# A weight fetch for a change of expert at step 23 moved to step 1 in a mixture-of-experts stage

## The chip, the cores and the metric

The kernel runs on one core of a Trainium2 chip, in one launch. The metric is the device time of that launch in microseconds (us). Below, PE is TensorE, DVE is VectorE, ACT is ScalarE, POOL is GpSimd and SP is SyncE, which in this kernel only issues transfers and waits.

## The reference, cut to what matters

The layer is a graph-attention stage, a linear-attention stage, and a mixture-of-experts (MoE) stage on 1250 rows of 768 columns. Only the last one matters here:

```python
probs = softmax(x @ router_w)                    # 8 experts
gates, idx = top_k(probs, 2)                     # 2 experts for each row
g = silu(x @ w_gate[e]);  u = x @ w_up[e]        # for every expert e, 768x768 each
expert_out = (g * u) @ w_down[e]
routed = sum over the two experts of gate * expert_out
shared = silu(x @ ws_gate) * (x @ ws_up) @ ws_down
out = x + alpha * shared + (1 - alpha) * routed
```

## The kernel before

The MoE stage works in 23 steps (`NTM`), numbered 0 to 22. The rows are sorted by expert into chunks of 64 slots, and each step takes two chunks at once, one in each half of the PE array. Half 0 runs through the experts from the front (it starts with expert 0), half 1 from the back (it starts with expert 7). Each half has its own set of three weight buffers of 2304 KB (gate, up, down): `ew[0][i]` and `ew[1][i]`, at the arena offsets `EW[i][0]` and `EW[i][1]`. The first six weights are fetched by `load_expert` (L616) while the shared part runs.

There are always seven changes of expert (`NB1`). DVE works out a table of them while the shared part runs: in `order_changes` it has for each change the step from which the new weights are needed (`cht`), the expert (`che`) and the half (`isr`), ranks the changes by step, and counts for each step how many changes are due by then. `list_changes` writes that count as `loads_i` (32 + 16 for each change due) and the sorted list as `change_i`, three rows of seven integers, in a loop of one pass per row (L1097 to L1101). PE takes `loads_i[j]` at the start of step j and waits for that value of `s_ew[0]` ahead of the gate products, `s_ew[1]` ahead of the up products, and `s_ew[2]` ahead of the down products; `s_ew[i]` rises by 16 with each landed weight of kind i.

A change whose `cht` is 23 belongs to a boundary between experts that falls right behind the last step of half 0. No step needs its weights, but they are fetched all the same, and waited for at the end of SP's program.

The order on SP, an in-order queue, is: the loads of the first weights, mixed with the stores of the ten groups of output rows (`store_rows`, L372; semaphore `s_fout`), two small loads of the slot table (L640, L641), the wait for `s_et` (the table of changes is there), and then the loop over the seven changes (L645 to L653). Each turn loads three integers into registers (L646 to L648), and for gate, up and down in turn waits for the weights of the turn before and for PE to have done with the old ones (L651: `s_g`, `s_up` or `s_y` at `at_step`), and issues the fetch (L652). Behind the loop SP waits for all weights, for `s_fout` and for the last row write.

POOL adds each chunk's rows into the output in DRAM: an indirect read of 64 rows (L690), DVE adds the products (L1156), an indirect write (L694), one chunk after the other, 46 in all but the last two, which share one read (L698) and one write (L701). DVE works in order too: `take_h(j+1)` (L1143), which PE needs for the turns (L797) in step j+1, stands behind the two `add_rows` of step j. The PE lines are L803 for all expert products (48 matmuls for each of gate, up, down as the trace counts them), L788 for the turns of x, L797 for the turns of h, L841 for the last step.

Of the kernel before, what the change touches and what calls it, by code (L numbers as in the profile page):

```python
# [24 lines left out]
I32 = mybir.dt.int32  # L25
U32 = mybir.dt.uint32
U16 = mybir.dt.uint16
ALU = mybir.AluOpType
# [7 lines left out]
ARENA = 52900  # L36
SMALL = 3456
# [19 lines left out]
def gps_layer(nc, x, src, dst, norm_g, norm_b, W1, a_src1, a_dst1, b1, W2, a_src2, a_dst2, b2, Wu, bu,  # L57
              w_qkv, w_proj, b_proj, router_w, w_gate, w_up, w_down, ws_gate, ws_up, ws_down, sg_w, sg_b,
              out):
    N, D = x.shape  # L60
    KD = D // P
    NT = 10
# [16 lines left out]
    NTM = -(-((2 * N + NE * (HP - 1)) // HP) // 2)  # L79
# [3 lines left out]
    with ExitStack() as ctx:  # L83
        def sem(name):
            return ctx.enter_context(nc.semaphore(name))

        arena = ctx.enter_context(nc.sbuf_tensor("arena", [P, ARENA], F32))
        ps = [ctx.enter_context(nc.psum_tensor(f"bank{i}", [P, 512], F32)) for i in range(8)]

        def words(off, n, dt=F32):  # L90
            v = arena[:, off:off + n]
            return v if dt == F32 else v.bitcast(dt)

        def region(at, size):

            pos = [SMALL + at]

            def take(n, dt=F32):
                w = n if dt in (F32, I32, U32) else (n + 1) // 2
                v = words(pos[0], w, dt)  # L100
                pos[0] += w
                assert pos[0] <= SMALL + at + size and pos[0] <= ARENA, (at, size, pos)
                return v
            return take
# [64 lines left out]
        COUNTS, MASK, V12, MIXT, XNT, ZB, END = 0, 6256, 12506, 20426, 27926, 35426, ARENA - SMALL  # L169
# [133 lines left out]
        EWW = KD * D  # L303
        EW = [(SMALL + WBO + i * EWW, SMALL + w) for i, w in enumerate((0, EWW, V12 + NT * D + KD * N + KD * HG - EWW))]
        assert NT * D <= 2 * EWW <= NT * D + KD * HS and 6 * D <= KD * N + KD * HG - EWW
        ew = [[words(EW[i][b], EWW).rearrange("p (k n) -> p k n", k=KD) for i in range(3)] for b in range(2)]
        sg_s = words(EW[2][0], NT * HS).rearrange("p (t n) -> p t n", t=NT)
        take = region(V12 + NT * D, KD * N)
# [5 lines left out]
        route = region(P - SMALL, D + G)  # L314
# [26 lines left out]
        NB1 = NE - 1  # L341
        NO = 4
        chs = route(NE)
        isr = route(NB1)
# [5 lines left out]
        cht = route(NB1)  # L350
        che = route(NB1)
        chk = route(NB1)
        chr_ = route(NB1)
        chc = route(NB1)
# [1 line left out]
        cho = route(NB1 * NB1).rearrange("p (r e) -> p r e", r=NB1)  # L356
        chv = route(NB1)
        stepw = route(NTM)
        change_i = route(3 * NB1, I32).rearrange("p (v r) -> p v r", v=3)
        loads_i = route(NTM, I32)  # L360

        info_last = route(2)
# [4 lines left out]
        tp, dv, sc, pl = nc.tensor, nc.vector, nc.scalar, nc.gpsimd  # L367
# [182 lines left out]
        s_ew = [sem(f"expert_w{i}_in") for i in range(3)]  # L550
# [13 lines left out]
        s_fout = sem("out_rows_written")  # L564
# [34 lines left out]
        def ffn_sync(sp):  # L599

            sp.wait_ge(s_ptused, NT * (H1 + H2))
            sp.wait_ge(s_fe, 2 * NF)
            sp.dma_start(wsg[:, :, HS:HS + NE], router_w.rearrange("(k p) n -> p k n", p=P)).then_inc(s_ws, 16)
            sp.dma_start(wsg[:, :, HS + NE:HG], sg_w.rearrange("(k p) n -> p k n", p=P),
                         allow_slow_non_contiguous=True).then_inc(s_ws, 16)
            sp.dma_start(wsg[:, :, 0:HS], ws_gate.rearrange("(k p) n -> p k n", p=P)).then_inc(s_ws, 16)
            sp.dma_start(wsd[:, :, :], ws_down.rearrange("(k p) n -> p k n", p=P)).then_inc(s_ws, 16)
            sp.wait_ge(s_zero, 16 * (NTM + 1))
            sp.dma_start(sgb[0:T], sg_b.partition_broadcast(T)).then_inc(s_sgb, 16)
            sp.wait_ge(s_fin, 2 * NT)  # L610
            sp.dma_start(wsu, ws_up.rearrange("(k p) n -> p k n", p=P)).then_inc(s_wsu, 16)

            def load_expert(b, i):

                w = (w_gate, w_up, w_down)[i]
                sp.dma_start(ew[b][i], w[(NE - 1) * b].rearrange("(k p) n -> p k n", p=P)).then_inc(s_ew[i], 16)  # L616

            load_expert(0, 0)
            load_expert(0, 1)

            def store_rows(t):
                sp.wait_ge(s_sout, 2 * (t + 1))
                rows_dma(sp, out_rows[:, t].rearrange("p (c n) -> p c n", n=FW), x2[0:T, t], s_fout)

            for t in range(2):
                store_rows(t)
            sp.wait_ge(s_rows, 16 * 2 * NT)
            load_expert(1, 0)
            for t in range(2, 4):
                store_rows(t)  # L630
            sp.wait_ge(s_sup, NT)
            load_expert(1, 1)
            load_expert(1, 2)
            sp.wait_ge(s_sh, NT)
            load_expert(0, 2)
            for t in range(4, NT):
                store_rows(t)
            sp.wait_ge(s_info, 16 * 2 * NT)
            sp.wait_ge(s_padout, 16)
            sp.dma_start(slot_info[0:HP], info_dram.rearrange("(j h p) c -> p j h c", h=2, p=HP)).then_inc(s_infoin, 16)  # L640
            sp.dma_start(info_last, info_dram[(NTM - 1) * P:NTM * P]).then_inc(s_infoin, 16)  # L641


            sp.wait_ge(s_et, 2)
            for c in range(NB1):  # L645
                at_step = sp.value_load(change_i[0:1, 0, c:c + 1], min_val=0, max_val=NTM)  # L646
                e = sp.value_load(change_i[0:1, 1, c:c + 1], min_val=0, max_val=NE - 1)
                b = sp.value_load(change_i[0:1, 2, c:c + 1], min_val=0, max_val=1)  # L648
                for i, (w, done, each) in enumerate(((w_gate, s_g, 2), (w_up, s_up, 2), (w_down, s_y, 1))):
                    sp.wait_ge(s_ew[i], 16 * (c + 2))  # L650
                    sp.wait_ge(done, at_step * each + 1)  # L651
                    sp.dma_start(arena[:, bass.ds(b * (EW[i][1] - EW[i][0]) + EW[i][0], EWW)].rearrange("p (k n) -> p k n", k=KD),  # L652
                                 w[bass.ds(e, 1)].rearrange("e (k p) n -> p (e k) n", p=P)).then_inc(s_ew[i], 16)  # L653
            for i in range(3):
                sp.wait_ge(s_ew[i], 16 * (NB1 + 2))
            sp.wait_ge(s_fout, 32 * NT)
            sp.wait_ge(s_accout, 16 * (2 * NTM - 1))

        def ffn_pool(pool):
# [242 lines left out]
        def ffn_dve(dve, step, add_out, mean_var):  # L902
            stt = dv.scalar_tensor_tensor
# [164 lines left out]
            def order_changes():  # L1068

                ids = iota[0:1, 1:NE]  # L1070
                step(dv.tensor_tensor(che[0:1], ids, isr[0:1], ALU.subtract))
                step(dv.tensor_scalar(chk[0:1], ids, -2.0, 15.0, ALU.mult, ALU.add))
                step.wait()
                step(dv.tensor_tensor(chk[0:1], chk[0:1], isr[0:1], ALU.mult))
                step.wait()
                step(dv.tensor_tensor(chk[0:1], chk[0:1], ids, ALU.add))
                step(dv.tensor_scalar(chc[0:1], cht[0:1], 16.0, None, ALU.mult))
                step.wait()
                step(dv.tensor_tensor(chk[0:1], chk[0:1], chc[0:1], ALU.add))
                step.wait()  # L1080
                step(dv.tensor_tensor(chm[0:1], chk[0:1].unsqueeze(1).to_broadcast([1, NB1, NB1]),
                                      chk[0:1].unsqueeze(2).to_broadcast([1, NB1, NB1]), ALU.is_lt))
                step(dv.tensor_tensor(stepm[0:1], cht[0:1].unsqueeze(1).to_broadcast([1, NTM, NB1]),
                                      iota[0:1, 0:NTM].unsqueeze(2).to_broadcast([1, NTM, NB1]), ALU.is_le))
                step.wait()
                step(dv.tensor_reduce(chr_[0:1], chm[0:1], AX.X, ALU.add))
                step(dv.tensor_reduce(stepw[0:1], stepm[0:1], AX.X, ALU.add))

            def list_changes():

                step.wait()
                step(dv.tensor_tensor(cho[0:1], chr_[0:1].unsqueeze(1).to_broadcast([1, NB1, NB1]),
                                      iota[0:1, 0:NB1].unsqueeze(2).to_broadcast([1, NB1, NB1]), ALU.is_equal))
                dv.tensor_scalar(loads_i[0:1], stepw[0:1], 16.0, 32.0, ALU.mult, ALU.add).then_inc(s_et, 1)
                for v, what in enumerate((cht, che, isr)):
                    step.wait()
                    step(dv.tensor_tensor(chm[0:1], cho[0:1], what[0:1].unsqueeze(1).to_broadcast([1, NB1, NB1]), ALU.mult))  # L1097
                    step.wait()
                    step(dv.tensor_reduce(chv[0:1], chm[0:1], AX.X, ALU.add))
                    step.wait()  # L1100
                    ins = dv.tensor_copy(change_i[0:1, v], chv[0:1])  # L1101
                    if v < 2:
                        step(ins)
                ins.then_inc(s_et, 1)

# [1390 lines left out]
```

## Time and profile before

| | us |
|---|---|
| time, median of 3 runs | 1650.14 (1647.8 to 1651.68) |
| time of the profiled execution | 1642.05 |
| its span, first to last instruction | 1640.0 |
| PE busy | 1555.6 (95%) |
| DVE busy | 811.2 (49%) |
| ACT busy | 335.1 (20%) |
| POOL busy | 250.7 (15%) |

The expert steps are the last 600 us of the span. Times in the rows below are from the start of the span. A row of the timeline reads: start, duration, engine, line, operation, destination and source, count, and in brackets how long the engine sat idle before it and what released it.

### The profile page before, as it was taken

What the parts mean: (1) busy time and instruction counts of PE and PEld (TensorE: products, weight loads), DVE (VectorE), ACT (ScalarE), POOL (GpSimd) and SP (SyncE); (2) the same over time, 40 slices, a digit from 0 to 9 for tenths busy, and PEclk for the clock granted to TensorE, in tenths of its full rate; (3) what the DMA queues carried; (4) which work ended last, traced back from release to release, by engine and by line L of the source; (5) the groups of instructions that cost most, each with busy time, mean ns of one, the idle gap of its engine ahead of it and who ended that gap; (6) DMA issues with size and microseconds to landing.
All of it is one profiled execution on the core that took longest, in us unless ns stands there. A gap on an engine that the chain in (4) does not pass through costs nothing.

```text
span 1640.0 us, 21951 instructions
## 1 busy us (share of the span) xinstructions
PE 1555.6 (95%) x8501; PEld 1034.3 (63%) x8502; DVE 811.2 (49%) x1539; ACT 335.1 (20%) x493; POOL 250.7 (15%) x234
## 2 busy tenths in 40 slices
PE   6999999999899999998989999999999999999995
PEld 4466666557779999998987555444444444444442
DVE  7545447998867899984887433111111111111111
ACT  2321112001223255560372110100100000001000
POOL 1087820000000000000000027111111111111111
PEclk9999999999999999999979999999999999999998
DMA  9900020000004536213111318925629211613415
GB/s 268 339 2 1 2 61 1 1 1 1 1 1 117 160 80 187 58 26 84 32 46 59 144 44 170 327 63 197 221 52 323 92 48 53 211 42 122 136 30 193
DMA packets 85337, 163.79 MB, mean 100 GB/s; under 512 B 18874, under 2 KB 48816, under 8 KB 85001
## 3 DMA queue, kind: packets, MB, share of 16 engines
q1 hardware_dynamic: 66903, 119.07, 22.6%
q0 software_dynamic: 12096, 23.27, 6.3%
q10 hardware_dynamic: 6258, 20.40, 4.6%
q8 instruction: 48, 0.79, 0.2%
q14 instruction: 32, 0.26, 0.1%
HBM read 127.75 MB, written 37.56 MB: 101 GB/s over the span
## 4 chain that ended last, share of the span: by engine, by line
PE 62%; DVE 11%; POOL 8%; DMA 7%; issue 6%; SPq 3%; ACT 1%; DVEq 1%; ACTq 0%; POOLq 0%
PE bank L803 28%; POOL slot_table L1312 7%; PE bank L1629 6%; PE bank L1667 5%; PE bank L1531 5%; PE bank L1588 3%; PE bank L713 2%; DVE arena L2388 2%; PE bank L1467 2%; SPq L372 2%; DVE arena L2357 2%; PE bank L1414 2%; PE bank L1715 1%; DMA arena<-out_dram,arena 1%; DVE arena L2333 1%
## 5 line engine op out<-in xcount | busy, mean ns | idle before, releaser
L803 PE MATMUL bank<-arena 128*64 128x384 f32 x3312 | 540.7, 488 | 2.3 <-DMA arena<-in_L_ffn_w_down_dram 1.7
L803 PEld LDWEIGHTS bank<-arena 128*64 128x64 f32 x3312 | 237.1, 137 | 294.2 <-issue 291.4
L1156 DVE SCALAR_TENSOR_TENSOR arena<-bank,arena 64x384 f32<-64x384 f32 x88 | 50.3, 610 | 355.2 <-DMA arena<-out_dram,arena 214.4
L1667 PE MATMUL bank<-arena 125*125 125x198 f32 (+1 forms) x1200 | 193.9, 323 | 11.0 <-DVE arena L2357 10.8
L1667 PEld LDWEIGHTS bank<-arena 125*125 125x125 f32 x1200 | 187.3, 198 | 15.5 <-DVE arena L2357 15.2
L1629 PE MATMUL bank<-arena 128*125 128x192 f32 x960 | 163.7, 328 | 4.7 <-DVE arena L2310 3.8
L1629 PEld LDWEIGHTS bank<-arena 128*125 128x125 f32 x960 | 157.6, 189 | 5.5 <-DVE arena L2310 4.1
L1312 POOL DMA_INDIRECT slot_table<-arena x80 | 110.1, 1376 | 104.5 <-issue 104.5
L2194 DVE TENSOR_TENSOR arena<-arena,bank 125x417 f32 x186 | 109.4, 588 | 27.2 <-PE bank L1467 18.9
L2388 DVE SCALAR_TENSOR_TENSOR arena<-arena 125x1250 f32<-125x1250 f32 x60 | 90.8, 1514 | 10.6 <-ACT arena L1904 10.6
L664 POOL MEMSET arena<- 1x2500 f32 x1 | 2.2, 2177 | 598.3 <-DVE arena L2340 598.3
L1531 PE MATMUL bank<-arena 128*125 128x396 f32 x240 | 92.9, 496 | 0.0
L886 ACT ACTIVATE arena<-bank 128x384 f32<-128x384 f32 x46 | 22.6, 491 | 337.1 <-PE bank L803 337.1
L1917 ACT ACTIVATE arena<-arena 125x1250 f32<-125x1250 f32 x60 | 74.7, 1245 | 81.9 <-DVE arena L2388 80.6
L1588 PE MATMUL bank<-arena 128*128 128x250 f32 x360 | 89.7, 374 | 1.7 <-DVE arena L2247 1.7
L2333 DVE CUSTOM_DVE_ANT_0 arena<-arena 125x1250 bf16<-125x1250 bf16 x60 | 86.6, 1453 | 6.1 <-DMA arena<-score_rows 6.1
L2357 DVE SCALAR_TENSOR_TENSOR arena<-arena 125x1250 f32<-125x1250 f32 x60 | 87.1, 1453 | 0.9 <-PE bank L1667 0.9
L1904 ACT ACTIVATE arena<-arena 125x1250 f32<-125x1250 f32 x60 | 79.5, 1335 | 31.9 <-DMA arena<-score_rows 24.4
L694 POOL DMA_INDIRECT out_dram<-arena x44 | 40.3, 917 | 298.0 <-DVE arena L1156 298.0
L1414 PE MATMUL bank<-arena 128*125 128x384 f32 x240 | 82.2, 496 | 0.0
L1443 PE MATMUL bank<-arena 128*125 128x384 f32 x240 | 80.4, 487 | 0.0
L1467 PE MATMUL bank<-arena 128*125 128x417 bf16 x186 | 65.1, 351 | 10.5 <-DVE arena L2184 10.3
(307 smaller groups left out, 1528.2 us busy)
## 6 DMA issues: line engine op xcount, KB each, us to landing
arena<-in_L_ffn_w_gate_dram SPq DMA_DIRECT2D x9, 2304.0 KB, 9.3
arena<-in_L_ffn_w_up_dram SPq DMA_DIRECT2D x9, 2304.0 KB, 10.6
arena<-in_L_ffn_w_down_dram SPq DMA_DIRECT2D x9, 2304.0 KB
arena<-score_rows ACTq DMA_DIRECT2D x18, 585.9 KB
expert_in<-arena SPq DMA_DIRECT2D x23, 384.0 KB, 9.6
arena<-expert_in ACTq DMA_DIRECT2D x23, 384.0 KB, 6.0
arena<-in_L_mix_w_qkv_dram SPq DMA_DIRECT2D x2, 2304.0 KB, 17.7
xn_columns<-arena SPq DMA_DIRECT2D x1, 3750.0 KB, 15.0
```

Of the source, the lines that this page charges most:

```text
L803: ins = tp.matmul(ps[bank][HP * h:HP * h + HP, 0:384], frm[:, b, k, HP * h:HP * h + HP], ew[h][i][:, k, n * 384:(n + 1) * 384], start=(k = ...
L1312: pl.indirect_dma_start(table_dram[:, :], bass.IndirectOffsetOnAxis(ap=slot_i[0:T, c:c + 1], axis=0), vhw[0:T, NTB * TC + c:NTB * TC + c + ...
L1414: ins = tp.matmul(ps[i % 2][0:T, 0:384], xnT[:, k, t * T:(t + 1) * T], wkv[:, 0, k, hf * 384:(hf + 1) * 384], start=(k == 0), stop=(k == K ...
L1467: tp.matmul(ps[6 + j % 2][0:T, 0:G], ohs[:, (j // OB) % 2, j % OB, :], ohd[:, j % 4, 0:G], start=True, stop=True).then_inc(s_cps, 1)
L1531: ins = tp.matmul(ps[q % 4][0:T, 0:2 * VW], xnT[:, k, t * T:(t + 1) * T], w12x[:, k, 2 * hf:2 * hf + 2, :], start=(k == 0), stop=(k == KD ...
L1588: ins = tp.matmul(ps[q % 2][:, 0:QN], wq[:, k, mb * P:(mb + 1) * P], xnT[:, k, g * QN:(g + 1) * QN], start=(k == 0), stop=(k == KD - 1))
L1629: ins = tp.matmul(ps[side_bank(u)][0:T, 0:FW], frm[:, k, t * T:(t + 1) * T], wchunk[:, c % 2, k, :], start=(k == 0), stop=(k == KD - 1))
L1667: ins = tp.matmul(ps[bank][0:T, c * width:(c + 1) * width], ptile[0:T, j % NPT, dt * T:(dt + 1) * T], values(n - first, st), start=(st == ...
L2194: dv.tensor_tensor(o, o, ps[6 + j % 2][0:T, 0:G], ALU.add).then_inc(s_acc, 1)
L2333: step(dv.tensor_tensor_reduce(junk[0:T, dt % 2], mask[0:T, dt], srowb[0:T, n % 2], 1.0, -3.0e38, ALU.add, ALU.max, smax[0:T, dt:dt + 1]))
L2357: stt(out=ptile[0:T, j % NPT], in0=tbuf[0:T, j % NTB3], scalar=1.0, in1=counts[0:T, st, 0:N], op0=ALU.min, op1=ALU.mult).then_inc(s_pt, 1)
L2388: stt(out=tbuf[0:T, j % NTB3], in0=abbuf[0:T, n % 2, 1], scalar=ssrc[:, st:st + 1], in1=tbuf[0:T, j % NTB3], op0=ALU.add, op1=ALU.max).the ...
```

## The change

The DVE table gets a flag `chu` for changes with `cht` at or above 23, and for those `cht` becomes 1. The list has five rows in place of three: step, expert, and one arena offset for each of gate, up, down, which for a flagged change lies in a spare stretch (`SPARE`; gate and down share one). SP loads five registers for a change, waits for `s_fout` ahead of the loop in place of behind it (the spare stretch overlaps the output rows), and ahead of a down fetch also waits until the gate weights of the same change have landed. `loads_i` is counted from the changed `cht`.

```diff
+        SPARE = [SMALL + 2 * EWW, SMALL + 3 * EWW, SMALL + 2 * EWW]
...
-        change_i = route(3 * NB1, I32).rearrange("p (v r) -> p v r", v=3)
+        chu = route(NB1)
+        change_i = route(5 * NB1, I32).rearrange("p (v r) -> p v r", v=5)
...
             sp.wait_ge(s_et, 2)
+            sp.wait_ge(s_fout, 32 * NT)
             for c in range(NB1):
...
-                b = sp.value_load(change_i[0:1, 2, c:c + 1], min_val=0, max_val=1)
+                to = [sp.value_load(change_i[0:1, 2 + i, c:c + 1], min_val=0, max_val=ARENA - EWW) for i in range(3)]
                 for i, (w, done, each) in enumerate(((w_gate, s_g, 2), (w_up, s_up, 2), (w_down, s_y, 1))):
                     sp.wait_ge(s_ew[i], 16 * (c + 2))
+                    if i == 2:
+                        sp.wait_ge(s_ew[0], 16 * (c + 3))
                     sp.wait_ge(done, at_step * each + 1)
-                    sp.dma_start(arena[:, bass.ds(b * (EW[i][1] - EW[i][0]) + EW[i][0], EWW)].rearrange("p (k n) -> p k n", k=KD),
+                    sp.dma_start(arena[:, bass.ds(to[i], EWW)].rearrange("p (k n) -> p k n", k=KD),
...
-            sp.wait_ge(s_fout, 32 * NT)
...
+                step(dv.tensor_scalar(chu[0:1], cht[0:1], float(NTM), None, ALU.is_ge))
+                step.wait()
+                step(stt(out=cht[0:1], in0=chu[0:1], scalar=1.0 - NTM, in1=cht[0:1], op0=ALU.mult, op1=ALU.add))
...
-                for v, what in enumerate((cht, che, isr)):
+                for v in range(5):
+                    what = (cht, che)[v] if v < 2 else chc
+                    if v >= 2:
+                        to = EW[v - 2]
+                        step(dv.tensor_scalar(chc[0:1], isr[0:1], float(to[1] - to[0]), float(to[0]), ALU.mult, ALU.add))
+                        step.wait()
+                        step(stt(out=chc[0:1], in0=chu[0:1], scalar=float(SPARE[v - 2] - to[0]), in1=chc[0:1],
+                                 op0=ALU.mult, op1=ALU.add))
```

## Rows read from the trace of the kernel before

**Rows 1.** Timeline of SP, 1050 to 1640 us: start, duration, line, operation, count
```profile
1049.84 15.22 SPq L372 DMA_DIRECT2D out_dram<-arena  x11
1065.16 0.95 SPq L640 DMA_DIRECT2D arena<-slot_info_rows  x1
1066.15 3.99 SPq L641 DMA_DIRECT2D arena<-slot_info_rows  x1
1103.07 0.44 SPq L652 DMA_DIRECT2D arena<-in_L_ffn_w_gate_dram  x1
...
1604.44 0.38 SPq L652 DMA_DIRECT2D arena<-in_L_ffn_w_gate_dram  x1
...
1621.33 0.38 SPq L652 DMA_DIRECT2D arena<-in_L_ffn_w_down_dram  x1
```

**Rows 2.** Chain that ended last, 1500 to 1640 us: start, us, what
```profile
1588.59 23.39 PE bank L803 x144
```

**Rows 3.** Line L83, the program's end: duration ns min/median/max, first and last start
```profile
L83 POOLq DRAIN  x1: 9054/9054/9054, 1630.7 to 1630.7; - x1
```

**Rows 4.** Timeline of POOL, 1620 to 1641 us
```profile
1624.84 1.03 POOL L701 DMA_INDIRECT out_dram<-arena  x1 [9.50 <-DVE arena L1170]
```

**Rows 5.** Line L701, the last row write: us from issue to landing
```profile
DMA to landing us min/median/max: 5.7/5.7/5.7
```

**Rows 6.** Line L694, the 44 row writes of the steps: us from issue to landing
```profile
DMA to landing us min/median/max: 2.0/2.9/6.3
```

**Rows 7.** Timeline of PE, 1042 to 1090 us: steps 0 and 1
```profile
1042.85 15.70 PE L803 MATMUL bank<-arena 128*64 128x384 f32 x96 [0.64 <-ACT arena L877]
...
1061.67 23.44 PE L803 MATMUL bank<-arena 128*64 128x384 f32 x144 [1.66 <-DMA arena<-in_L_ffn_w_down_dram]
1085.65 0.55 PE L797 MATMUL bank<-arena 128*128 128x128 f32 x3 [0.54 <-DVE arena L1143]
```

**Rows 8.** SP's register loads by line: ns min/median/max, first and last start
```profile
L646 SPq TENSOR_LOAD <-arena x7: 262/270/487, 1070.2 to 1522.6; - x7
...
L648 SPq SEQ_ASSERT  x7: 18/18/18, 1072.1 to 1524.2; - x7
```

**Rows 9.** A window of 1 us; last three columns: granted clock, DMA share, GB/s
```profile
1069.00:1070.00 1.00, 1.00 (x8) 0.43 (x6) 0.00 (x0) 0.00 (x0) 0.00 (x0) 1.00 0.21 16
```

**Rows 10.** Line L652, the 21 fetches of the loop: us from issue to landing
```profile
DMA to landing us min/median/max: 8.7/9.4/11.2
```

**Rows 11.** Windows of 1 us: PE busy (count) first; last three columns as above
```profile
230.00:231.00 1.00, 0.95 (x3) 0.98 (x4) 0.95 (x2) 0.00 (x0) 0.00 (x0) 0.50 1.03 418
235.00:236.00 1.00, 1.00 (x5) 1.00 (x4) 0.52 (x2) 0.00 (x0) 0.00 (x0) 0.50 0.00 0
...
1264.00:1265.00 1.00, 1.00 (x6) 0.36 (x6) 0.56 (x1) 0.26 (x1) 0.00 (x0) 0.50 1.06 427
```

**Rows 12.** Timelines of POOL, DVE and PE where two changes come in consecutive steps
```profile
1253.03 0.95 POOL L690 DMA_INDIRECT arena<-out_dram,arena  x1 [5.72 <-DMA out_dram<-arena]
...
1260.62 1.16 DVE L1156 SCALAR_TENSOR_TENSOR arena<-bank,arena 64x384 f32<-64x384 f32 x2 [15.06 <-DMA arena<-out_dram,arena]
...
1262.42 0.55 PE L797 MATMUL bank<-arena 128*128 128x128 f32 x3 [2.87 <-DVE arena L1143]
...
1264.24 24.72 PE L803 MATMUL bank<-arena 128*64 128x384 f32 x144
```

**Rows 13.** Chain that ended last, 1068 to 1090 us: step 0's first read and write
```profile
1072.46 3.41 DMA arena<-out_dram,arena
...
1078.00 2.96 DMA out_dram<-arena
```

**Rows 14.** Timeline of DVE around `list_changes`: starts of two passes, the next shared tile
```profile
995.88 0.20 DVE L1097 TENSOR_TENSOR arena<-arena 1x49 f32<-1x49 f32 x1
...
996.53 0.20 DVE L1097 TENSOR_TENSOR arena<-arena 1x49 f32<-1x49 f32 x1
...
999.41 0.56 DVE L983 TENSOR_TENSOR arena<-bank,arena 125x384 f32<-125x384 f32 x1 [1.51 <-PE bank L732]
```

More of the change, by code:

```diff
@@ L305, in gps_layer @@
         assert NT * D <= 2 * EWW <= NT * D + KD * HS and 6 * D <= KD * N + KD * HG - EWW
+        SPARE = [SMALL + 2 * EWW, SMALL + 3 * EWW, SMALL + 2 * EWW]
+        assert 4 * EWW <= V12 + NT * D
         ew = [[words(EW[i][b], EWW).rearrange("p (k n) -> p k n", k=KD) for i in range(3)] for b in range(2)]
@@ L1101, in list_changes @@
                     ins = dv.tensor_copy(change_i[0:1, v], chv[0:1])
-                    if v < 2:
+                    if v < 4:
                         step(ins)
```

## The prediction, made before the changed kernel ran

> **What bounds the kernel now.** I began at the end, with the timeline of SP, to see whether the fetch in question is there. The loop makes 21 fetches, the last gate fetch at 1604.44 and the last down fetch at 1621.33 us [rows 1]. The chain that ended last has one run of 144 products from 1588.59 [rows 2]: 48 down products of step 21, 48 gate and 48 up products of step 22, 7.8 us each. So step 22's gates end at 1588.59 + 2 x 7.8 = 1604.2, and the fetch at 1604.44 follows them: it is a change at step 23, whose weights nobody uses. The change does have an object on this data.
>
> Next, what ends the program. Line L83 shows that POOL's closing DRAIN starts at 1630.7 and takes 9.05 us [rows 3]; that gives 1639.75, the end of the span of 1640.0 but for a barrier. The drain follows the landing of the last row write, issued at 1624.84 [rows 4] and landed 5.7 us later, at 1630.5 [rows 5]. The last weight fetch, issued at 1621.33, keeps SP waiting until 1630.7 as well (9.4 us), but SP has no long drain behind it. So the fetch matters at the end mostly through what it does to the row write: the 44 writes of the steps before take 2.0 to 6.3 us, median 2.9, most of them with no fetch beside them [rows 6].
>
> Last, the other end of the stage, where the fetch goes. PE has hardly a gap there: step 0's gate and up products run from 1042.85, and the run from 1061.67 holds step 0's down products and then, at once, step 1's gates and ups [rows 7]. By 7.81 us for each 48, step 1's gates start at 1061.67 + 7.8 = 1069.5, its ups at 1077.3, and its down products at about 1087.2. SP's timeline [rows 1] shows the other queue in question: stores of output rows until 1065.06, then L640 and L641 until 1070.14, and only then the loop.
>
> **Removed: the fetch behind the last step.** The last row write has no rival for the DMA engines. Its landing falls from 5.7 to 2.9 us [rows 5, 6], and everything behind it moves up: a gain of 2.8 us. SP's own wait goes too, and is not late next: POOL's drain is. Bounds: 0, if the drain's 9.05 us is no fixed price and ends when it did; and 3.7, if the write lands as the fastest of the 44 does, in 2.0. I take 2.8, by the median.
>
> **Added: a wait in step 1.** `cht` becomes 1, so `loads_i[1]` is 48 and PE waits in step 1, ahead of the gates, for a gate fetch that did not exist. The question is when that fetch is issued. SP's condition on PE (`s_g` at 3, step 0's gates) was met at 1042.85 + 7.8 = 1050.7 [rows 7], but SP isn't there. It comes to the loop at 1070.14. The new wait for `s_fout` costs nothing or little: the DMA engines are at 0.21 of their time from 1069 to 1070 [rows 9], so the stores, queued ahead of L641, have about landed. If not, they have by the landing of L641's own load at 1071.5, which bounds this at +1.3. Then the registers: three loads take from 1070.2 to 1072.1 [rows 8], some 0.6 us each; five take until 1073.3. With the last address arithmetic the gate fetch is issued at about 1073.6. The 21 fetches of the loop took 8.7 to 11.2 us to land, median 9.4 [rows 10]: it lands at 1083.0 (1082.3 to 1086).
>
> PE would have begun those gates at 1069.5. It stands still for 13.5 us (12.8 to 16.5), at a place where nothing covers it, since PE's program is in order. This is the main term.
>
> One rule of the Trainium skill gives another price for it. The page DMA: Bandwidth & Descriptors, section Anatomy of one DMA, has a fixed 2.0 us plus bytes over 436 GB/s: for 2304 KB that is 7.4 us, an estimate from the page. The sum would then be 2.0 us less. The 21 fetches here never landed under 8.7, so the trace doesn't agree for this path, and the rows stand.
>
> **Up and down.** The up fetch is issued some 0.5 us behind the gate fetch (its conditions are long met), and the two share the engines. A fetch at 400 GB/s needs 5.9 us of them, so up lands near 1089 to 1090. PE wants it at 1083.0 + 7.8 = 1090.8 at full clock, later at half. Down is issued when the gate weights have landed, the new extra wait, at 1083; it lands by 1083 + 11.2 at most plus the rest of up, by about 1096, and is wanted at 1083.0 + 15.6 + 1.5 = 1100.1. Both are hidden, up by a small margin; if it isn't, 1 to 3 us come on top. What is queued behind that extra wait on SP is the change at step 3, which is due at about 1103 and later: free.
>
> **The clock.** After a long idle stretch PE works at half clock. After the gap before 1262.42 [rows 12] the clock is 0.50, the lower level of 1.2 GHz, at 1264 [rows 11], and the next 144 products take 24.72 us in place of 23.44: 1.3 us more; the turns before take 1.8 (1262.42 to 1264.24) in place of 1.5, so 1.6 in all. Elsewhere the lower level holds from before 230 until after 235 us with PE busy [rows 11]: more than 6 us at half speed, some 3 to 3.5 us lost. PE stands still here for far longer than in either, so it will be at the lower level when it starts again. I take 2.5, from 1.6 to 3.5.
>
> **What the stall hides or worsens.** Before, step 1's turns of h waited 0.54 us for DVE [rows 7], which sat behind POOL's chain of read, add, write, read for step 0 [rows 13]. With PE later, that is gone: -0.5. But the chain now runs beside three fetches: under two changes in a row a read took from 1253.03 to 1260.6, 7.6 us, and PE lost 2.87 [rows 12]. At such prices the chain from 1072.46 is: read 7.6, add and issue 2.1, write 6.3, issue 0.8, read 7.6, add 1.2, so DVE is free at about 1098, and `take_h` gives the first half at 1098.6. PE wants it at 1083.0 + 15.6 + 2.5 = 1101. Hidden by the stall itself; without it, up to 3 us.
>
> **DVE and register work, costed at nothing.** `list_changes` grows by two passes, 0.65 us each (995.88 to 996.53), and six small operations, about 0.2 each; `order_changes` by two. That is 2.5 us before L983 of the next tile, which now waits 1.51 for PE [rows 14]. L983 comes 1.0 us late. It feeds turns that PE makes two tiles later, over 7 us on, so nobody waits; if that cover were gone, 1.0 us. The two more registers in each of the other six turns of the loop are loaded while SP waits tens of us for PE.
>
> **Sum.** 13.5 + 2.5 - 0.5 - 2.8 = +12.7 us. The span becomes 1652.7, and the profiled time 1642.05 + 12.7 = 1654.8. That execution is 8.1 us (0.5%) below the median of 1650.14, and the edit touches nothing that differs between them, so I add the sum to the median: 1662.8.
>
> **Rivals.**
> 1. Forecast: the fetch comes too late for step 1. +12.7, with bounds of 12.8 + 1.6 - 0.5 - 3.7 = +10.2 and 16.5 + 3.5 - 0.5 = +19.5. Chance 0.80.
> 2. The same, with a second wait behind the first (up late, or the row chain late, or both by 3): 1666 to 1670. For it: the margin of up is a microsecond. Against it: half clock gives the margin another 2.5. Chance 0.12.
> 3. The other side: the fetch is in time and only the gain at the end is left, 1650.1 - 2.8 = 1647.3. It takes a gate fetch issued by 1069.5 - 9.4 = 1060.1, thus 13.5 us earlier than SP's queue allows; it decides for a gain once the issue comes within 2 us of that. The L372 and L641 rows until 1070.14 [rows 1] speak against it. Chance 0.04. The Trainium skill, page DMA: Bandwidth & Descriptors, says in its Rules for kernel authors to issue a transfer early, compute, and wait late; read as a verdict on this edit it would make this rival the forecast. Here the wait is moved with the issue, and the rows put it ahead of the landing.
> 4. It doesn't do what it says, or gain and loss meet: PE isn't held by the extra count, or by a few microseconds only. Within 3.3 us of 1650.1. Nothing in the code speaks for it, as `loads_i` is counted from the changed step. Chance 0.04.
>
> A measurement of this kernel can tell about 0.2%, 3.3 us, from no change. Cases 1 and 2 are slower: 0.92; case 4 is the same: 0.04; case 3 is faster: 0.04. The range takes in cases 1 and 2, and at its lower end a run spread of 2 us beside the fixed bounds: 1657 to 1670.
>
> **What would show it.** Right: in the profile after, three L652 rows from about 1073.6 with the first three in 10 us, a gap of 13 to 14 us on PE ahead of step 1's gates put down to the gate weights, clock 0.50 behind it, no L652 row behind the change at step 19, L701 landing in about 3 us, and POOL's drain still 9 us long. Wrong: if the first L652 row stands well before 1070 (SP's queue misread), if the PE gap is under 8 us, if the drain grows by what the write gains, or if a second gap follows in step 1. Step 0's wait of 1.66 us for the down weights and the gap at 1262 should stay as they are.

## The result, and the profile after

The changed kernel takes 1656.12 us (median of 14 runs, 1652.01 to 1660.14), the kernel before 1648.01 us in 14 runs of its own (1642.65 to 1651.68). The ratio is 1.0052, with a 95% interval of 1.004 to 1.0064: slower by 8.6 us (6.6 to 10.5). The forecast was slower by 12.7 us, 1662.8 us in all, with a range from 1657.0. The direction was right, and the time is 0.9 us below the range.

The profiled execution has a span of 1656.8 us. SP's timeline after, from the first of the stores behind the weights to the second change (start, duration, engine, line, operation, count), answers to [rows 1]:

```profile
1050.98 21.29 SPq L377 DMA_DIRECT2D out_dram<-arena  x12
1072.37 0.88 SPq L645 DMA_DIRECT2D arena<-slot_info_rows  x1
1073.28 3.25 SPq L646 DMA_DIRECT2D arena<-slot_info_rows  x1
1079.94 0.44 SPq L660 DMA_DIRECT2D arena<-in_L_ffn_w_gate_dram  x1
1080.64 0.39 SPq L660 DMA_DIRECT2D arena<-in_L_ffn_w_up_dram  x1
1088.73 0.39 SPq L660 DMA_DIRECT2D arena<-in_L_ffn_w_down_dram  x1
1124.52 0.39 SPq L660 DMA_DIRECT2D arena<-in_L_ffn_w_gate_dram  x1
```

The last slot table load ends at 1073.28 + 3.25 = 1076.53, and the gate fetch is issued 3.41 us later. The down fetch is issued only when the gate weights have landed. PE's timeline after, steps 0 and 1, answers to [rows 7]:

```profile
1047.41 7.96 PE L810 MATMUL bank<-arena 128*64 128x384 f32 x48 [1.16 <-DMA arena<-in_L_ffn_w_gate_dram]
1056.76 7.96 PE L810 MATMUL bank<-arena 128*64 128x384 f32 x48 [1.38 <-DMA arena<-in_L_ffn_w_up_dram]
...
1068.62 7.96 PE L810 MATMUL bank<-arena 128*64 128x384 f32 x48 [2.44 <-DMA arena<-in_L_ffn_w_down_dram]
1088.56 18.66 PE L810 MATMUL bank<-arena 128*64 128x384 f32 x96 [11.98 <-DMA arena<-in_L_ffn_w_gate_dram]
1107.15 0.55 PE L804 MATMUL bank<-arena 128*128 128x128 f32 x3
```

What was one run of 144 products is cut in two: 48 down products of step 0, then 11.98 us of nothing, put down to the gate weights, and then 96 products that take 18.66 us where 96 took 15.7 before [rows 7]. Windows after (first the stretch and its length, then PE busy; last three: granted clock, DMA share, GB/s), answering to [rows 11]:

```profile
1087.00:1090.00 3.00, 1.44 (x6) 0.72 (x8) 0.00 (x0) 0.00 (x0) 0.00 (x0) 0.50 1.02 400
1090.00:1093.00 3.00, 3.00 (x12) 1.19 (x10) 0.00 (x0) 0.00 (x0) 0.95 (x1) 0.50 1.04 409
1093.00:1096.00 3.00, 3.00 (x16) 1.41 (x14) 0.00 (x0) 0.35 (x1) 0.00 (x0) 0.74 1.03 395
```

The products start at half clock and are back at the full one in the third window. The end after, the last row write (timeline of POOL), its landing, and POOL's drain (by line), answers to [rows 3 to 5]:

```profile
1644.47 1.03 POOL L708 DMA_INDIRECT out_dram<-arena  x1 [12.71 <-DVE arena L1187]
...
DMA to landing us min/median/max: 2.9/2.9/2.9
...
L83 POOLq DRAIN  x1: 9054/9054/9054, 1647.5 to 1647.5; - x1
```

The write lands in 2.9 us in place of 5.7, and the drain is as long as it was to the nanosecond.

A measure that leaves out what differs ahead of the change is the time from the start of step 1's gates (or the end of step 0's down products, where there is a gap) to the end of the span. It is 1640.0 - 1069.5 = 570.5 us before and 1656.8 - 1076.4 = 580.4 after: +9.9. The spans themselves differ by 16.8 us. The other 6.9 lie ahead of that point: PE began step 0's turns of x 4.0 us later, and waited for more of the first weights in step 0. Over the ten profiles of this document those turns began between 1039.7 us (the kernel with the longer table and without the move) and 1045.4 us (here), with 1042.9 in a kernel without any part of the change. So the profiles do not tie these 6.9 us to the change, and the timed difference, 8.6 us, is too small to hold them on top of the 9.9.

### The profile page after: what moved, and what is told of

Its sections match the earlier page's. It is cut to its first block, busy times and chain, and to the rows that moved or that the text cites. A ratio compares the mean times of both kernels' runs of the same rounds, so it can differ in the third digit from the quotient of the medians.

```text
span 1656.8 us, 22015 instructions
## 1 busy us (share of the span) xinstructions
PE 1559.1 (94%) x8501; PEld 1037.7 (63%) x8502; DVE 814.1 (49%) x1553; ACT 335.6 (20%) x493; POOL 250.8 (15%) x234
## 4 chain that ended last, share of the span: by engine, by line
PE 68%; DVE 10%; POOL 7%; issue 5%; DMA 5%; SPq 3%; ACT 1%; DVEq 1%; ACTq 0%; POOLq 0%
PE bank L810 30%; POOL slot_table L1329 7%; PE bank L1646 6%; PE bank L1684 5%; PE bank L1548 5%; PE bank L1605 3%; PE bank L720 2%; DVE arena L2405 2%; PE bank L730 2%; PE bank L1484 2%; DVE arena L2374 2%; PE bank L1431 2%; SPq L377 2%; PE bank L748 2%; PE bank L1732 1%
## 5 line engine op out<-in xcount | busy, mean ns | idle before, releaser
L701 POOL DMA_INDIRECT out_dram<-arena x44 | 40.3, 917 | 308.8 <-DVE arena L1173 308.8
L1160 DVE TENSOR_TENSOR arena<-bank,arena 128x384 f32<-128x384 f32 x46 | 25.6, 558 | 109.6 <-PE bank L810 109.4
## 6 DMA issues: line engine op xcount, KB each, us to landing
expert_in<-arena SPq DMA_DIRECT2D x23, 384.0 KB, 10.2
xn_columns<-arena SPq DMA_DIRECT2D x1, 3750.0 KB, 15.1
```

## The experiments

All but the two repeats were also timed against the kernel before; their ratios stand with 95% intervals.

**The same fetch at step 2.** One number:

```diff
-                step(stt(out=cht[0:1], in0=chu[0:1], scalar=1.0 - NTM, in1=cht[0:1], op0=ALU.mult, op1=ALU.add))
+                step(stt(out=cht[0:1], in0=chu[0:1], scalar=2.0 - NTM, in1=cht[0:1], op0=ALU.mult, op1=ALU.add))
```

> The changed kernel with one number different: a flagged change gets step 2 in place of step 1. Theory (the loss is PE waiting in step 1 for a fetch that SP, late in its queue, can only issue some 3.5 us behind PE's arrival): SP now waits for step 1's gates and issues at once, step 2's gates come 17 us later, so the wait of 12.0 us and the 3.0 us at half clock go. The 2.8 us at the end stay gained. But now changes at steps 2 and 3 follow each other, which may bring a row-chain stall of up to 4 us as in step 9. Expected against the kernel before: -2.8 to +2 us, ratio 0.998 to 1.001. Rival A (a third weight fetch near the start costs by itself, by its traffic, wherever it stands): ratio stays near 1.005. Rival B (the longer table, the moved wait for stores and the two extra registers cost): ratio stays near 1.005 too.

Measured: 1.0024 (1.0009 to 1.0039), +3.9 us. PE's timeline, its rows with a gap in steps 1 and 2:

```profile
1091.32 0.90 PE L804 MATMUL bank<-arena 128*128 128x128 f32 x3 [3.64 <-DVE arena L1160]
1119.40 0.55 PE L804 MATMUL bank<-arena 128*128 128x128 f32 x3 [1.74 <-DVE arena L1160]
```

No gap in steps 1 and 2 is put down to a weight any more, so the 12 us did come from the wait in step 1. But it is no gain either, and 1.9 us above the upper end of what I had expected (+2, which the interval, from +1.5 us, still holds). The fetches now stand directly ahead of those of step 3, and PE waits 3.64 and 1.74 us for DVE, with half clock behind the first, which costs 1.4 us by the durations of the turns and products. Measured like the 9.9 us above, this profile is 3.5 us longer than that of the kernel before. Rivals A and B, with a ratio near 1.005, are out: 1.005 lies outside the interval.

**Issued at step 1, waited for at step 2.** In `order_changes` the flagged `cht` is 2 while the count for PE is made, and 1 in SP's list:

```diff
-                step(stt(out=cht[0:1], in0=chu[0:1], scalar=1.0 - NTM, in1=cht[0:1], op0=ALU.mult, op1=ALU.add))
+                step(stt(out=cht[0:1], in0=chu[0:1], scalar=2.0 - NTM, in1=cht[0:1], op0=ALU.mult, op1=ALU.add))
...
                 step(dv.tensor_reduce(stepw[0:1], stepm[0:1], AX.X, ALU.add))
+                step.wait()
+                step(stt(out=cht[0:1], in0=chu[0:1], scalar=-1.0, in1=cht[0:1], op0=ALU.mult, op1=ALU.add))
```

> The changed kernel, the fetch issued at the same point (step 1), but the count that PE waits for rises only with step 2. Theory: the PE gap of 12.0 us ahead of step 1's gates goes with the wait alone, and the half clock behind it (3.0 us). The traffic of three fetches is still in step 1, now beside a PE that does not stand still: step 1's turns of h may wait up to 3 to 10 us for DVE behind the row chain (a read of 7.6 us under traffic in place of 3.4 and 2.0), since the chain then ends at about 1098 on the old time axis and step 1 wants h at 1085. Expected: +1 to +9 us in that wait, -2.8 at the end; ratio 0.999 to 1.004. Rival A (only the semaphore wait costs, traffic is free): ratio 0.998. Rival B (the cost is in the table or the stores' wait): ratio near 1.005.

Measured: 1.002 (1.0004 to 1.0036), +3.3 us. The traffic stands where the change put it and only the wait is gone. The chain of work that ended last (start, us, what) shows what comes in its place:

```profile
1081.05 6.98 DMA out_dram<-arena
...
1088.86 5.25 DMA arena<-out_dram,arena
...
1095.32 0.57 DVE arena L1162
1095.89 0.04 issue
1095.93 0.90 PE bank L804 x3
```

A row write takes 6.98 us and a read 5.25 beside the fetches, where [rows 13] have 2.96 for the same write. DVE's `take_h` stands behind them and PE waits in front of step 1's turns of h; PE's timeline:

```profile
1095.93 0.90 PE L804 MATMUL bank<-arena 128*128 128x128 f32 x3 [7.53 <-DVE arena L1162]
...
1098.68 24.34 PE L810 MATMUL bank<-arena 128*64 128x384 f32 x144
```

So three fetches in step 1 cost two things. The larger, 12 us, hides the smaller, 7.5 us: take the semaphore wait away, and DVE's is next. Measured like the 9.9 us above, this profile is 5.6 us longer than that of the kernel before, near the upper end of the timed interval (0.7 to 5.9). Rival A (traffic is free, 0.998) is outside the interval, and so is rival B.

**The longer table without the move.** The changed kernel with `scalar=0.0` in that line, so the flagged change stays at step 23 (it still goes into the spare stretch).

> The changed kernel with its longer table, five registers, spare stretch and earlier wait for the stores, but the flagged change keeps step 23. Theory (these parts cost nothing): ratio 1.000 within 0.1%, PE's shared stage without a new gap, the fetch again behind step 22, last row write 5.7 us, POOL's drain 9.05 us. Rival (the table or the moved wait costs): ratio 1.001 to 1.003, with a gap of 1 to 3 us on PE near the shared tiles.

Measured: 0.9988 (0.9968 to 1.0008). In its profile the last write lands in 5.1 us again. The table, five registers, the spare stretch and the earlier wait for the stores cost nothing that can be seen; a cost of 1 us is within the interval, one of 2 us is not.

**No fetch at all.** The kernel before with `for c in range(NB1 - 1)` in SP's loop and `16 * (NB1 + 1)` in the waits behind it: the fetch for step 23 is left out.

> The kernel before with SP's loop one turn shorter, so that the fetch behind the last step isn't made at all and isn't waited for (on this data no step uses it). It measures the gain at the end by itself. Theory: the last row write lands in 2.9 us in place of 5.7, the drain stays 9.05: -2.8 us, ratio 0.998. Rival (the drain ends at a time of its own, or the write doesn't gain): ratio 1.000.

Measured: 0.9986 (0.9973 to 0.9999), -2.3 us. The last write and the drain, timeline and line:

```profile
1625.38 1.03 POOL L701 DMA_INDIRECT out_dram<-arena  x1 [12.42 <-DVE arena L1170]
...
L83 POOLq DRAIN  x1: 9054/9054/9054, 1628.5 to 1628.5; - x1
```

The drain starts 3.1 us behind the issue, in place of 1630.7 - 1624.84 = 5.9. That is the gain of 2.8 us at the end by itself.

**The same fetch at step 12.** The same line with `12.0 - NTM`.

> The changed kernel, a flagged change gets step 12 in place of step 1: its three fetches stand between the changes at steps 9 and 15, with no neighbour within two steps, and SP has long been waiting there. Theory (two prices at step 1: PE waits for a late fetch, or, without that wait, DVE's row chain beside the traffic of three fetches holds the turns of h up): a single change that stands alone brings no gap on PE, as those at 3, 5, 15 and 19 do not. So only the gain at the end is left, about -2.3 us as without the fetch: ratio 0.9975 to 0.9995, no PE gap in steps 11 to 13. Rival (any additional fetch within the steps costs about as much as its place at step 2 did, +3.9 us): ratio 1.001 to 1.003, with a gap near step 12.

Measured: 0.9978 (0.9959 to 0.9997), 1641.41 us: faster than both kernels. Its three fetches are issued at 1331.94, 1339.69 and 1348.99, PE has no gap between the one in step 9 and the last step, and the last write lands in 2.9 us. The idea of the change gives its 2.8 us where the moved fetches stand alone (timed: 3.6, from 0.5 to 6.7); it is the place that costs.

**The first fetch later.** In SP's loop, behind the five registers:

```diff
+                for _ in range(10 if c == 0 else 0):
+                    sp.value_load(change_i[0:1, 0, c:c + 1], min_val=0, max_val=NTM)
```

> The changed kernel, SP loads ten more integers ahead of the first fetch of its loop, 0.55 to 0.6 us each, so the fetch at step 1 is issued about 5.8 us later. Theory (PE's gap is issue plus landing minus PE's arrival, with nothing else to cover it): the gap ahead of step 1's gates grows one for one, from 12.0 to about 18 us; ratio about 1.0085. Rival (the gap is set by something else that ends at that time, such as traffic of the stores or the slot table): the gap stays at 12 and the ratio at 1.005.

Measured: 1.0077 (1.0047 to 1.0108). PE's timeline:

```profile
1063.89 9.65 PE L812 MATMUL bank<-arena 128*64 128x384 f32 x48 [2.06 <-DMA arena<-in_L_ffn_w_down_dram]
1088.74 17.30 PE L812 MATMUL bank<-arena 128*64 128x384 f32 x96 [15.20 <-DMA arena<-in_L_ffn_w_gate_dram]
```

The gap grew to 15.2, not 18. The ten loads put the issue at 1080.06, which is 8.8 us behind the end of the last slot table load (1071.2) in place of 3.4, so 5.4 later. But PE came 2.3 us behind that end (1088.74 - 15.20 = 1073.54), where in the changed kernel it came with it (1076.58 against 1076.53). Of these 2.3 us, 1.7 are step 0's down products, which took 9.65 us in place of 7.96. 12.0 + 5.4 - 2.3 = 15.1, as the gap. The sum of the expectation holds, with PE's arrival as its other end. The timed ratio agrees with a longer gap, but its interval touches that of the change, so the gap in the trace is what this rests on.

**Second profiles of both kernels.**

> The changed kernel unaltered, for a second profile: how far the terms differ from one execution to the next. Theory: the gap ahead of step 1's gates is set by two in-order queues and stays at 12.0 within 1 us, the half clock behind it costs 2 to 3.5, and the gap in step 9 (2.4 to 2.9) is there with 0 to 1.6 us of half clock behind it, by chance. Rival (the change removed the half clock behind step 9's gap): no half clock there again.

> The kernel before unaltered, for a second profile. Theory: the gap of step 9 is there again (2.3 to 3.1 us), and the half clock behind it costs anything from 0 to 1.6 us; step 1's gates start within 1 us of the end of SP's last slot table load. Rival (the 1.3 us of slow products in step 9 belong to the kernel before): 24.7 us for these 144 products again.

The changed kernel again, PE's timeline:

```profile
1063.27 7.96 PE L810 MATMUL bank<-arena 128*64 128x384 f32 x48 [1.60 <-DMA arena<-in_L_ffn_w_down_dram]
1082.66 18.45 PE L810 MATMUL bank<-arena 128*64 128x384 f32 x96 [11.43 <-DMA arena<-in_L_ffn_w_gate_dram]
...
1277.71 0.55 PE L804 MATMUL bank<-arena 128*128 128x128 f32 x3 [2.77 <-DVE arena L1160]
...
1279.17 23.44 PE L810 MATMUL bank<-arena 128*64 128x384 f32 x144
```

The kernel before again:

```profile
1059.44 23.44 PE L803 MATMUL bank<-arena 128*64 128x384 f32 x144 [0.83 <-DMA arena<-in_L_ffn_w_down_dram]
...
1260.24 0.89 PE L797 MATMUL bank<-arena 128*128 128x128 f32 x3 [3.52 <-DVE arena L1143]
...
1262.98 23.78 PE L803 MATMUL bank<-arena 128*64 128x384 f32 x144
```

The gap of step 1 is 11.43 (11.98 in the first), and the products behind it take 18.45 us (18.66). From step 1's gates to the end it is 579.9 us for the changed kernel (580.4) and 1637.7 - 1067.2 = 570.5 for the one before (570.5). Two pairs, +9.4 and +9.9.

Step 9 has to be read with its turns. In the kernel before, turns and products behind the gap take 1.82 + 24.72 us in [rows 12] and 2.74 + 23.78 here (1262.98 - 1260.24, then the products). At full clock they take 1.46 + 23.44. So the half clock costs 1.6 us in both profiles, only split otherwise, and the gap of 3.52 is above the 2.3 to 3.1 that I had expected. In the changed kernel the rival came true: no half clock, as in its first profile:

```profile
1283.50 0.55 PE L804 MATMUL bank<-arena 128*128 128x128 f32 x3 [2.45 <-DVE arena L1160]
...
1284.96 23.44 PE L810 MATMUL bank<-arena 128*64 128x384 f32 x144
```

The delayed kernel, with a longer gap in step 1, has the half clock in step 9 again:

```profile
1282.55 0.55 PE L806 MATMUL bank<-arena 128*128 128x128 f32 x3 [2.68 <-DVE arena L1162]
...
1284.77 24.31 PE L812 MATMUL bank<-arena 128*64 128x384 f32 x144
```

It is there in all eight profiles of the other kernels and in neither of the changed one. Whether that is chance or the change is not shown.

## Why the prediction was right or wrong

**The mechanism held.** The fetch comes too late for step 1 because SP is still busy with stores and the slot table, PE stands still, starts again at half clock, and gets 2.8 us back at the end. Removing the wait alone, moving the fetch to steps 2 or 12, and delaying it each moved the gap as this says. What failed is the size of the main term.

**SP's issue: right.** Foreseen 3.5 us behind the end of L641; it was 3.41 and 3.42.

**PE's gap: 13.5 foreseen, 12.0 and 11.4 measured; the step that failed most.** Two readings made it too long. The landing was taken as the median of the fetches in the loop, 9.4 [rows 10]; it was 8.5, below the fastest of the 21 at 8.7. Why is not shown: it too ran beside a row read (issued at 1079.07, landed in 3.6 us) and the start of a row write (1084.76), and from 0.7 us on beside the up fetch. The 8.7 was the fastest of one execution; a later fetch of the changed kernel landed in 8.3. The 7.4 us that the prediction works out from the Trainium skill (DMA: Bandwidth & Descriptors, section Anatomy of one DMA) is too short by 1.1; the fit there is given for transfers issued from GpSimd, and SP issues these. And PE's head start over SP was read from one execution: 1070.14 - 1069.5 = 0.65 us. In the four executions of the two kernels it was 0.65, -0.5 (1066.8 against 1067.2), 0.1 and -0.5: PE's step 0 is itself held by weights from the same queue, so the two ends move together, but not to the tenth. My lower bound of 12.8 lay above both gaps.

**Half clock: 2.5 foreseen, 3.0 and 2.8 measured** (18.66 and 18.45 against 15.7), 1.6 in the delayed kernel.

**Step 1's wait for DVE: -0.5 foreseen, and gone** (the second profile of the kernel before has none to lose). DVE was free at 1097.6, and its `take_h` waited for PE's products until 1103.5. What it would cost without the cover I put at up to 3 us. That does not follow from the prediction's own chain: it has the first half of h at 1098.6, where step 1 of the kernel before wants it at 1085.1, 13.5 us earlier. With the wait removed it was 7.5. The reads took 4.1 and 5.3 us and not 7.6 each, the write 7.0 (6.3 foreseen); h was there some 23 us behind step 1's start, and PE wants it after 16.

**The end: -2.8 foreseen, -2.8 measured**, by the write's landing, and a gain of 2.3 (0.2 to 4.4) timed by itself. Against it stand 0.35 us that nobody had in the sum: PE's last products (L848) start 9.04 us behind the start of step 22's down products, in the kernel before (L841) 8.69 us. It is so in six of the seven profiles with the longer table, and its cause is open.

**Costed at nothing.** The table and the registers: right in sum. `list_changes` grew by 2.4 us, about as foreseen (1000.94 to 1005.3, where it took from 995.88 to 997.9 before): L990 of the next tile started at 1005.25 while PE had been ready since about 1004.3, and PE had no gap there.

**What was not foreseen.** In the first pair, step 9's gap and the clock behind it took 4.6 us before and 2.5 after (the excess of two steps over 24.83 us each). Summed: 12.1 (PE's arrival to its start) + 3.0 - 0.5 - 2.8 + 0.35 - 2.1 = +10.0, against 9.9 by the spans. Over ten profiles of all kernels here this item ran from 2.5 to 6.9 us, the two smallest (2.5 and 2.8) in the two profiles of the changed kernel. Whether the change has a part in that stays open; the delayed kernel, with a longer gap in step 1, shows 4.4.

**The range.** It failed at its lower end for two reasons. Its terms added up to at least +10.2, where the timed difference is 8.6 (6.6 to 10.5). And it stood on the median of three runs, 1650.1; fourteen runs have 1648.0, with 9 us between the fastest and the slowest. I had allowed 2. (The bounds as written give 1650.1 + 10.2 - 2 = 1658.3; the 1657 has 1.3 us more for which no term is given.) With either put right, 1656.1 lies inside: with the base of fourteen runs the range begins at 1654.9, with the measured gap of 11.4 as its lower bound at 1655.6. The centre's error of 6.7 us is 2.1 of base, 2.8 of terms (12.7 against 9.9), and 1.8 that lies within the interval.

The rivals: the second wait (case 2) did not come on top: the gap gave the row chain time, and the up weights landed 6.3 us behind the gate weights (1094.7 against 1088.4), where PE wants them after 7.8 at the earliest. The fetch in time (case 3) is what step 12 shows, at 0.9978.

## What to carry to other kernels

A transfer moved to an idle place is moved with its wait: compare the issue time that its queue allows, not the time from which its data may be fetched, with the first instruction that counts on it. If the wait is a running count shared by all transfers, even data that nobody uses stops the engine. And look for the second price under the first: here small row transfers on the same DMA engines, held up by the big ones, were the next thing to be late, and a place three steps away from any other fetch had neither.

## What the runs showed of the hardware

- POOL's closing DRAIN behind indirect transfers took 9054 ns in each of the ten profiles. It starts when the last row write has landed, so each microsecond of that landing is one of the time.
- A fetch of 2304 KB with no other fetch in flight at its issue landed in 8.5 us, one issued 0.7 us behind it in 14.1, and the third, issued at the first's landing, in 11.9: they share about 400 GB/s (395 to 409 in the windows from 1087 to 1096 us).
- An indirect row write, 2.9 us in the median, took 5.1 to 7.0 us beside such fetches in step 1 and at the end.
- Gaps of 2.3 to 4.5 us on PE in step 9 were followed by half clock in eight of ten profiles, at a cost of 1.6 to 2.4 us; after gaps of 2.45 and 2.77 us the clock stayed at the full level, and after one of 2.28 it fell. The length of the gap alone does not decide it.
